# A prefetch hint for the closing branch of the hop loops, on all five engines of a graph kernel

## What is computed

```python
def step(f, _):
    msg = f[src] * edge_weight[:, None]
    agg = jax.ops.segment_sum(msg, dst, num_segments=n)
    f = (1.0 - ALPHA) * agg + ALPHA * feat_0
    return (f, None)
out, _ = jax.lax.scan(step, feat, None, length=K)   # K = 10
```

## Time and profile before

| what | value |
|---|---|
| median of 3 runs | 11055.2 us (11045.51 to 11082.27) |
| the profiled execution, its own time | 11089.94 us |
| its span | 11088.1 us |
| one hop (L1272 from branch to branch) | about 458 us, (6816.2 - 2694.3) / 9 |
| busy share of the span | PE 83%, PEld 69%, DVE 63%, POOL 43%, ACT 41% |
| mean granted TensorE clock | 0.925 |

### The profile page before, as it was taken

How to read it: one execution, slowest core, us unless ns; L and a number is a source line. 1 busy time by engine, 2 the same in 40 slices (tenths; PEclk the granted TensorE clock), 3 DMA queues, 4 the chain that set the end, 5 groups by cost and what they waited for, 6 DMA issues and landing times. The chain is left out here.

```text
span 11088.1 us, 570048 instructions
## 1 busy us (share of the span) xinstructions
PE 9243.7 (83%) x240266; PEld 7632.4 (69%) x240266; DVE 7022.9 (63%) x16172; ACT 4528.6 (41%) x8837; POOL 4781.5 (43%) x4058
## 2 busy tenths in 40 slices
PE   5886766788888888888888886999999999958585
PEld 4665656777878778778787785666666666658485
DVE  7998978877777777777777776222222222267377
ACT  2333988943333333333333332443434344323132
POOL 0000000055555555555555554655555555335053
PEclk9998995599999999999999998999999999979598
DMA  3000014588888878878888885111111111048085
GB/s 27 0 0 0 0 18 193 227 275 271 281 268 270 283 260 284 267 262 280 270 275 265 272 279 167 21 20 20 20 20 20 20 20 20 12 161 283 23 274 167
DMA packets 479754, 1689.66 MB, mean 152 GB/s; under 512 B 166486, under 2 KB 227950, under 8 KB 477550
## 3 DMA queue, kind: packets, MB, share of 16 engines
q1 hardware_dynamic: 412926, 1632.87, 44.5%
q0 software_dynamic: 59776, 46.03, 2.8%
q10 hardware_dynamic: 6640, 4.93, 0.2%
HBM read 1521.16 MB, written 157.36 MB: 151 GB/s over the span
## 5 line engine op out<-in xcount | busy, mean ns | idle before, releaser
L1144 POOL TENSOR_TENSOR arena<-arena 128x768 f32<-128x768 f32 (+2 forms) x1800 | 2714.0, 1508 | 1938.6 <-DVE arena L1198 1931.8
L1128 ACT CAST arena<-banks 128x384 bf16<-128x384 f32 (+1 forms) x3600 | 1951.7, 607 | 3430.2 <-DVE banks L1194 3424.6
L1239 PE MATMUL banks<-arena 32*128 32x144 bf16 x118800 | 2300.8, 225 | 398.3 <-DVE arena L1166 287.1
L1227 PE MATMUL banks<-arena 128*128 128x48 bf16 x58800 | 2512.4, 184 | 1.4 <-issue 1.4
L1227 PEld LDWEIGHTS banks<-arena 128*128 128x128 fp8e4 x58800 | 2357.6, 96 | 16.7 <-issue 16.7
L1227 PE MATMUL banks<-xc,arena 128*128 128x48 bf16 x24500 | 2069.0, 185 | 328.2 <-DVE arena L1198 113.2
L1239 PEld LDWEIGHTS banks<-arena 32*128 32x128 bf16 x118800 | 1947.0, 92 | 519.8 <-DVE arena L1166 297.8
L1227 PEld LDWEIGHTS banks<-xc,arena 128*128 128x128 fp8e4 x24500 | 1917.0, 96 | 515.4 <-issue 309.2
L1198 DVE TENSOR_TENSOR arena<-banks,arena 128x384 f32<-128x384 f32 (+1 forms) x3600 | 1904.2, 567 | 354.2 <-ACT arena L1128 354.2
L1419 POOL DMA_INDIRECT f<-node_table,idx x1568 | 1580.9, 1008 | 1207.7 <-ACT idx L1434 759.4
L1194 DVE TENSOR_TENSOR banks<-banks,wslot 128x384 f32<-128x384 f32 (+1 forms) x3600 | 1874.7, 567 | 355.4 <-PE banks L1227 353.7
(11 more groups left out here) (315 smaller groups left out, 12206.7 us busy)
## 6 DMA issues: line engine op xcount, KB each, us to landing
arena<-onehots SPq DMA_DIRECT2D x1200, 768.0 KB, 4.4
arena<-onehots SPq DMA_DIRECT2D x300, 864.0 KB, 4.4
arena<-onehots SPq DMA_DIRECT2D x300, 800.0 KB, 4.3
onehots<-arena SPq DMA_DIRECT2D x100, 768.0 KB, 3.3
node_table<-xc SPq DMA_DIRECT2D x11, 2352.0 KB, 17.6
f<-node_table,idx POOLq DMA_INDIRECT x1568, 2.4
onehots<-arena SPq DMA_DIRECT2D x25, 864.0 KB, 3.5
onehots<-arena SPq DMA_DIRECT2D x25, 800.0 KB, 3.3
```

What stands on the lines that cost most here:

```text
L1128: m = nc.scalar.copy(as_bank(mp_b[:, b % 3, 0, tiles, :, 1]), bank)
L1144: nc.gpsimd.tensor_tensor(mp[:, b % 3, 2, 0:NTILE[b], :], mp[:, b % 3, 1, 0:NTILE[b], :], mp_b[:, b % 3, 1, 0:NTILE[b], :, 1], ALU.subtrac ...
L1227: m = nc.tensor.matmul(to, hot[:, i * P:(i + 1) * P], x_part, start=c == 0, stop=c == 2)
L1239: m = nc.tensor.matmul(banks[:, 4 + q, 0:3 * D], hot[rows, i * P:(i + 1) * P], mp_b[rows, b % 3, :, i, :, 1], start=b == 0 and i == 0, sto ...
```

## The change

A helper makes the five loops of `spmm`. The loops stay as they were, except that `Fori` is told to mark a hint location as the first instruction of the body on its engine, and to tie the closing branch to it.

```diff
+        def looped(eng, start, end):
+
+            return nc.Fori(start, end, engines=(eng.engine,), hint_back_edge=True)
+
...
-                    with sp.Fori(1, NGRP) as d:
+                    with looped(sp, 1, NGRP) as d:
...
-                    with act.Fori(0, NGRP) as d:
+                    with looped(act, 0, NGRP) as d:
...
-                    with pool.Fori(0, NGRP // OVR) as t:
+                    with looped(pool, 0, NGRP // OVR) as t:
...
-                    with dve.Fori(1, NGRP // OVR) as t:
+                    with looped(dve, 1, NGRP // OVR) as t:
...
-                    with pe.Fori(0, NGRP - 1) as d:
+                    with looped(pe, 0, NGRP - 1) as d:
```

## The result

The changed kernel takes 11103.28 us (median of 5 runs, 11095.14 to 11108.24) against 11055.2 us before (now 5 runs, 11045.51 to 11082.27). The ratio is 1.0036, with a 95% interval from 1.0019 to 1.0052: slower by 21 to 57 us. The time lies in the forecast's range; the likeliest case, 3 to 32 us with 13 in its middle and "no change" as the reading, was not what happened: the medians lie 48 us apart. The profiled execution spans 11102.0 us, only 13.9 us more than that of before, but that one lay 35 us above its median, and this one lies on it. So one span against the other doesn't give the size.

The account below looks back on a forecast made before the run. The prediction took a ring to bound the kernel: DVE from overflow tile to batch 2, POOL, the indirect transfer, DVE again. No saving, other hints hidden, DVE's 13 us: 11055.2 + 13 = 11068 us, range 11040 to 11112.

Parts of the forecast that it names:

- the likeliest case: DVE's hint exposes 0.01 to 0.11 us per turn, 3 to 32 us in all, 13 expected; chance 0.66.
- The saving, put at nothing: At the five loops' closing branches: none waits for instructions, PE's taking 215 ns, so hints save nothing.
- DVE's term: Between batch 5's last subtraction and batch 0's first multiply, DVE's hint exposes 0.045 us per turn, 288 times: 13 us.
- the price: What the hint takes on DVE's sequencer at the loop's head: 0.075 us, within 0.04 to 0.2 us.
- the cover: Part of DVE's hint hidden under the subtraction still running across the branch: 0.03 us.
- The hints of ACT, POOL and SP, put at nothing: At the loop's head these engines stand waiting, 1.7, 1.2 and 2.1 us each, so their hints are hidden.
- PE, 288 times: hidden: PE's hint ahead of batch 2's gather only shortens the following 1.09 us wait for DVE; hidden if under about 1 us.
- rival 2: PE's hint loses read-ahead of the tail behind the loop: 3.1 us per exit, 12 times, 37 us; chance 0.06.
- Rows 8: Profile rows of queue traffic over 350 us of turns, 3230 to 3580: no instruction packet fetched, so loop code is resident.
- Its high end of 11112 us: Range's top: dear DVE hint (11104) or lost PE read-ahead with DVE's term (11105), plus some 7 us of scatter.
- the 11103 that the prediction gives from the profiled execution's own time: The same 13 us added to the profiled execution's 11089.94 us instead of the median: 11103 us.

Follow-up runs that it names:

- e2: The hint on DVE's loop alone, none on the other four engines, against the kernel before: 11251.22 us, ratio 1.0006 (0.9997 to 1.0015).
- g2: The hint on ACT's loop alone, against the kernel before: 11252.68 us, ratio 0.9997 (0.9988 to 1.0006).
- f1: The hint on PE's loop alone, at the head of the body, against the kernel before: 11285.83 us, ratio 1.0016 (1.0007 to 1.0025).
- f4: The kernel before, unchanged, measured and profiled again on the same chip as a reference: 11263.13 us, ratio 0.9999 (0.9990 to 1.0008).
- e3: The hint on PE, ACT, POOL and SP, none on DVE, against the kernel before: 11290.78 us, ratio 1.0041 (1.0026 to 1.0056).
- f2: The hint on ACT, POOL and SP, none on PE and DVE, against the kernel before: 11270.34 us, ratio 1.0004 (0.9995 to 1.0013).
- the first set: Four kernels timed in rounds against the kernel before: the whole change, DVE's hint alone, all but DVE's, and DVE's moved later; ratios 1.0006 to 1.0043.
- e4: All five hints, DVE's moved from the loop's head to ahead of batch 4, against the kernel before: 11277.97 us, ratio 1.0035 (1.0022 to 1.0048).
- e1: The change itself once more, all five hints, against the kernel before: 11292.49 us, ratio 1.0043 (1.0028 to 1.0058).
- the second set: Four kernels timed against the kernel before: PE's hint alone; ACT, POOL and SP's; PE's hop branch hinted instead; no change; ratios 0.9998 to 1.0016.
- in the third: Four kernels timed against the kernel before: PE's hint late, ACT's alone, POOL and SP's alone, PE's ahead of the loop; ratios 0.9995 to 1.0016.
- g1: The hint on PE alone, marked late in the body at batch 5, against the kernel before: 11266.41 us, ratio 1.0016 (1.0007 to 1.0026).
- g4: The hint on PE alone, marked ahead of the loop instead of in it, against the kernel before: 11247.78 us, ratio 0.9995 (0.9986 to 1.0004).
- f3: No hint in the five loops; PE's closing branch of the hop loop hinted instead, against the kernel before: 11264.42 us, ratio 0.9998 (0.9989 to 1.0007).

## Why the prediction was right in its range and wrong in its case

- **The saving, put at nothing: right.** PE's closing branch got no shorter, and its loop held one fetch, early in the hop, and none in the turns behind it.
- **DVE's term, 0.045 us a turn: right**, in size (46 ns) and in both of its parts: 0.075 us taken as the price, 78 ns measured, and 0.03 us as the cover, 32 ns measured. The price was a choice within wide bounds, 0.04 to 0.2 us, so that it came so near is in part luck. Its sum of 13 us isn't shown as a sum: e2 measured 7 us (-3 to 17).
- **The hints of ACT, POOL and SP, put at nothing: ACT's right** (g2), and right in the turns for all three. The hints of POOL and SP together make ACT's first copy 0.7 us later at each start of a hop; what that costs is not shown.
- **"PE, 288 times: hidden": this is the step that failed.** I costed PE's hint as an instruction that takes time, and in the turns that costs nothing: DVE's quiet turns are as short in f1 as in f4 (16.80 us both). It also acts on what is fetched, and its price of nothing left out 1.8 us at each of 12 exits, 22 us. I had this as rival 2 with a chance of 0.06. Its ground against it was "the loop's head is resident, so there is nothing to turn the fetcher for". The runs showed that the head's being there doesn't protect: with the hint in the turns, the loop no longer has its one fetch ahead, and the tail has one more (fetches of tail and loop 4 and 1, then 5 and 0).
- **Rival 2's price was too high:** 3.1 us per exit as a whole fetch not covered; it measured 1.8 us in f1, and I take it that most of the additional fetch goes by under the block that runs. Its total of 11105 us, with DVE's term, is near the measured 11103 partly by luck.
- **Rows 8 misled me a little.** They showed no instruction fetch in 350 us of turns, from 3230 on. The one that mattered starts at 3209.6, about when the loop's second closing branch is taken, just ahead of them.
- **That the time lies in the range is in part luck.** Its high end of 11112 us came from the rivals, not from the forecast. And the 11103 that the prediction gives from the profiled execution's own time equals the measured median only because that execution lay 34.7 us above its own.

The parts found, as the profiles price them: DVE 13 us, PE's tail 1.8 x 12 = 22 us, the hop starts 0.7 x 9 = 6 us. Together 41 us, 0.37%, and 0.36% and 0.43% were measured. Of the three, the time of a run alone shows only PE's. The single runs add up to less: 0.06 + 0.16 + 0.04 = 0.26%, each with 0.09 of uncertainty. And e3 (0.41%) is above f1 and f2 together (0.20%). A part of that is visible in the first set's profiles, outside the changed loops: the edge layer between the tenth hop and the third layer's sum takes 3275 us in e2, and 3281 to 3296 us in e4, e3 and e1. Other profiles speak against a share of the change in it: it takes 3302 to 3306 us in all four of the second set; in the third 3294 us in g1, with PE's hint, and 3302 to 3304 in the other three (one of them, g4, with PE's hint ahead of the loop); and on the first chip 3020 us before and 3019 after. In the changed kernel's own profile, on the first chip, the tail grew by only 0.95 us a sum (17.84 to 18.79).

What stays open: which of POOL's and SP's hints delays ACT's start and how; why a hint to a block that is there moves the fetch from the loop to the tail, as the counts show that it does; and the rest between the parts and the whole.

No version here beats both kernels: the best hint placement (f3, g4) is as fast as none.

## What to carry to other kernels

Ask first whether a closing branch waits at all: 0.2 us against 3.7 us is seen at once in the row of its source line, and then whether anybody waits for that engine (f3 took 3.2 us off a branch nine times and gained nothing). A hint is not only an instruction to be costed at its length: here it changed what was fetched when, so what runs behind the loop belongs in its price. And where a chain runs through an engine's sequencer, as DVE's here, its cover can be read from the rows, and the exposed rest is then the price of every turn, as far as longer turns for other reasons don't take it up.

## What the runs showed of the hardware

A hint takes 31 ns on four engines and 39 ns on DVE, in its row. On DVE it held the sequencer up by 78 ns, of which 32 were hidden and 46 lengthened the step. A hinted branch to code that isn't there falls from 3637 to 412 ns on PE (f3), about 200 ns above one whose target is there (216 ns). I hadn't expected that a hint for a target already there costs the code behind the loop one more fetch, 1.8 us per exit at the head of the body (f1) and 1.3 late in it (g1, 19.1 against 17.8), and nothing when run only once ahead of the loop (g4); nor that ACT's first instruction behind its hop branch would come 0.7 us later by hints on POOL and SP alone.

The Trainium skill (Runtime: NRT & Kernel Launch, Instruction fetch mechanics) calls the read-ahead purely sequential and driven by the sequencer. The traces are in keeping with that for the unhinted loop, where one block was fetched at about the second closing branch and the tail then had one fetch fewer; with the hint in PE's turns (f1, g1) the loop had no such fetch.
